# Up projections of a two-layer float32 transformer: each 512-column product issued as two halves of 256 columns

## The reference

```python
xn = layernorm(x)
x = x + L0_attn(xn) + L0_ffn(xn)   # causal attention, 32 heads of 16, 8 key/value heads, rotary
xn = layernorm(x)
x = x + L1_attn(xn) + L1_ffn(xn)   # causal sigmoid(4 * scores) without a softmax, 4 heads of 128

# L0_ffn, width 1792: each weight is multiplied elementwise by a product of rank 4
w_eff = w * (su @ sv)
out = down(silu(x @ gate_eff.T) * (x @ up_eff.T))
# L1_ffn, width 1376: the weight plus twice a product of rank 16
g = silu(lora(x, w1)) * lora(x, w3);  out = lora(g, w2)
```

## Time and profile before

| what | value |
|---|---|
| median of 3 timed executions | 708.31 us (707.09 to 709.48) |
| the profiled execution's own time | 710.41 us |
| its span, first to last instruction | 708.7 us |
| mean granted TensorE clock | 0.986 |
| matmuls recorded | 3606, as many weight loads |

### The profile page before, as it was taken

One profiled execution on the slowest core, in us unless ns is written; L12 is line 12 of the kernel. 1 busy time (PEld: TensorE's weight loads), 2 busy tenths in 40 slices (PEclk: granted clock), 3 DMA queues, 4 the chain that ended last, 5 costly groups with the idle time before them and its releaser, 6 DMA issues. The chain is left out here.

```text
span 708.7 us, 10147 instructions
## 1 busy us (share of the span) xinstructions
PE 684.1 (97%) x3606; PEld 518.3 (73%) x3606; DVE 417.5 (59%) x985; ACT 293.0 (41%) x552; POOL 236.5 (33%) x241
## 2 busy tenths in 40 slices
PE   8998999999999999999999999959999999999998
PEld 7787566666666666666687778847888788888886
DVE  6735865776767675566267662087666565565511
ACT  4212354555555544454434422245443344442321
POOL 4474022232222231222234625423233222322443
PEclk9998999999999999999999999978999999999999
DMA  9428714223313331321144520040010000102011
GB/s 290 116 89 226 153 32 123 69 73 92 74 44 74 74 74 44 74 79 57 43 141 156 181 86 0 1 122 31 31 59 31 31 30 31 60 30 60 16 59 60
DMA packets 23146, 55.19 MB, mean 78 GB/s; under 512 B 3732, under 2 KB 4088, under 8 KB 22040
## 3 DMA queue, kind: packets, MB, share of 16 engines
q1 hardware_dynamic: 22840, 54.41, 27.1%
q10 hardware_dynamic: 256, 0.13, 0.1%
HBM read 42.86 MB, written 11.54 MB: 77 GB/s over the span
## 5 line engine op out<-in xcount | busy, mean ns | idle before, releaser
L954 DVE CUSTOM_DVE_ANT_0 bank<-bank,mask 128x512 f32<-128x512 f32 (+3 forms) x256 | 118.4, 523 | 64.1 <-PE bank L1008 63.8
L214 POOL TENSOR_TENSOR up_w_lo<-up_w_eff,up_w_hi 128x512 fp32r<-128x512 f32 x50 | 65.8, 1323 | 123.0 <-ACT up_w_hi L210 122.9
L52 PE MATMUL bank<-x0T_hi,up_w_hi 128*128 128x512 f32 x224 | 96.9, 433 | 3.0 <-POOL up_w_lo L214 2.3
L383 POOL TENSOR_TENSOR down_h_lo<-hidden,down_h_hi 128x512 fp32r<-128x512 f32 x50 | 65.7, 1316 | 95.0 <-ACT down_h_hi L378 95.0
L908 ACT ACTIVATE probs<-bank 128x512 f32<-128x512 f32 x160 | 85.4, 597 | 28.5 <-PE bank L1030 25.8
L54 PE MATMUL bank<-x0T_lo,up_w_hi 128*128 128x512 f32 x224 | 89.5, 399 | 0.0
L53 PE MATMUL bank<-x0T_hi,up_w_lo 128*128 128x512 f32 x224 | 89.3, 399 | 0.0
L873 POOL TENSOR_SCALAR_AFFINE_SELECT probs<-probs 128x512 f32<-128x512 f32 x64 | 39.9, 635 | 124.3 <-ACT probs L908 124.1
L52 PE MATMUL bank<-down_w_hi,down_h_hi 128*128 128x512 f32 x200 | 78.3, 392 | 0.4 <-DVE bind_cols L1282 0.4
L53 PE MATMUL bank<-down_w_hi,down_h_lo 128*128 128x512 f32 x200 | 78.1, 390 | 0.0
L54 PE MATMUL bank<-down_w_lo,down_h_hi 128*128 128x512 f32 x200 | 78.0, 390 | 0.0
(11 more groups left out here) (144 smaller groups left out, 1277.4 us busy)
## 6 DMA issues: line engine op xcount, KB each, us to landing
w_raw<-in_w_gate_up SPq DMA_DIRECT2D x25, 512.0 KB, 4.2
w_raw<-in_w_down SPq DMA_DIRECT2D x25, 256.0 KB, 2.8
q_stack<-q_hi SPq DMA_DIRECT2D x32, 128.0 KB, 3.4
att<-att_T SPq DMA_DIRECT2D x16, 256.0 KB, 2.1
q_hi<-rope_hi SPq DMA_DIRECT2D x8, 256.0 KB
q_lo<-rope_lo SPq DMA_DIRECT2D x8, 256.0 KB
q_stack<-q_lo SPq DMA_DIRECT2D x16, 128.0 KB, 3.6
attention_or_xn<-att SPq DMA_DIRECT2D x16, 128.0 KB
```

What stands on the lines that cost most here:

```text
L52: pe.matmul(out, w_hi, m_hi, start=first, stop=False, skip_group_check=True)
L214: pool.tensor_tensor(self.half(self.w_lo[:, o % 2], k), self.half(self.w_eff, k), f32(self.half(self.w_hi[:, o % 2], k)), ALU.subtract).th ...
L383: pool.tensor_tensor(self.h_lo[:, k % 2, :], self.hid[:, o, b * S:(b + 1) * S], f32(self.h_hi[:, k % 2, :]), ALU.subtract).then_inc(self.h ...
L954: dve.tensor_tensor_reduce(out=own, in0=own, in1=e.mask[:, S - w:S], scale=1.0, scalar=NEG, op0=ALU.add, op1=ALU.max, accum_out=rmax[:, i, ...
```

## The change

A new helper `three_pass_halves` calls `three_pass` twice, first for the columns 0 to 255 of the bank and of the moving operand, then for 256 to 511, with the same stationary operands. Both versions of `pe_product` call it. Only the very first matmul of a bank keeps the flag `start`, and both halves carry `stop` at the end; the semaphore is raised by the last matmul of the second half.

```diff
+def three_pass_halves(pe, out, w_hi, w_lo, m_hi, m_lo, first, last):
+
+    for half in (slice(0, S // 2), slice(S // 2, S)):
+        done = three_pass(pe, out[:, half], w_hi, w_lo, m_hi[:, half], m_lo[:, half], first and half.start == 0, last)
+    return done
...
-        last = three_pass(pe, self.product_bank(o, b, k)[:, :], self.w_hi[:, o % 2, c, k, :], self.w_lo[:, o % 2, c, k, :],
-                          self.xT_hi[:, c, b * S:(b + 1) * S], self.xT_lo[:, c, b * S:(b + 1) * S],
-                          c == 0, c == NC - 1)
+        last = three_pass_halves(pe, self.product_bank(o, b, k)[:, :], self.w_hi[:, o % 2, c, k, :], self.w_lo[:, o % 2, c, k, :],
+                                 self.xT_hi[:, c, b * S:(b + 1) * S], self.xT_lo[:, c, b * S:(b + 1) * S],
+                                 c == 0, c == NC - 1)
```

## The result

The changed kernel takes 716.07 us (median of 4, 714.86 to 717.64) against 707.78 us for the kernel before in the same series. The ratio is 1.0115, with a 95% interval of 1.0083 to 1.0147. A second series of five executions beside thirteen of the kernel before gave 1.0121 (1.0102 to 1.0139). The forecast was 717.5 us and +9.2 us; measured are +8.3 and, from the second ratio, +8.6 us. The profiled execution took 714.96 us, its span is 713.2 us.

What follows compares the result with a forecast made beforehand. PE issuing matmuls back to back was taken to bound the kernel; +4.0 us (layer 0) + 5.7 (layer 1) - 0.5 (hidden) = +9.2 us on 708.31, so 717.5 us, 8-in-10 range 711.0 to 725 us.

Steps and rivals of the forecast that it cites:

- The bound: PE issues matmuls one behind the other, so a change in their distance reaches the end nearly in full; waits 16.6 us.
- The distance, 0.120 us: In long runs of up-projection halves, each 256-column matmul takes 0.120 us, so 0.240 us per former pass.
- the doubt about runs of three: Layer 1's three narrow passes show 0.117 us each, but a debt of 0.02 us may fall on the wide passes behind.
- the upper end, 0.123: A half in the up projections costs 0.123 us if the debt counts; the sum is then +16.7 us, 725 us.
- The small price: Rival: halves keep 0.117 us, layer 0 pays nothing, layer 1 +2.6 us, 710.6 us in all; chance 0.12.
- the faster way: Rival: halves in both layers go at the loads' 0.112 us, giving 699 us; chance 0.06.
- the slow pace in full: Rival: halves inherit layer 0's excess of 21 ns per matmul, 0.128 us each in both layers, 736 us; chance 0.06.
- the estimate from it: By the skill's issue-gap formula, halves cost 2.6 ns more per pass over 1179 passes, +3.1 us, 711.4 us.
- Layer 0, +4.0 us: 660 up-projection passes of layer 0 go from 0.234 to 0.240 us each, +4.0 us.
- Layer 1, +5.7 us: 519 up-projection passes of layer 1 go from 0.229 to 0.240 us each, +5.7 us.
- The hidden part, -0.5 us: PE's DMA waits absorb lost time: 0.3 us at five for `minus_max_rows`, 0.2 us at three for `weights_lo`.
- The lower clock: At 1.2 GHz halves cost nothing extra: 12 passes in layer 0 and 9 in layer 1 count 0.

Runs made afterwards that it cites:

- the down-projection run: Up projections whole again, the 600 passes of the two down projections in two pieces of 256 columns instead; 715.66 us, ratio 1.0104 to the kernel before.
- quarters: The changed kernel with each up product cut into four pieces of 128 columns instead of two of 256, 4800 matmuls; four executions took 1065.6 to 1095.3 us.
- thirds: The changed kernel with each up product cut into pieces of 172, 170 and 170 columns, 3600 matmuls; 851.75 us, ratio 1.2024 to the kernel before.

## Why the prediction was right

**The bound.** PE issues back to back and the end follows it: the price of halves in one layer, in the other and in the down projections each arrived at the end. The prediction's 16.6 us of waits are those of the six rows shown; all twelve in the list add up to 20.9 us, which changes nothing in the argument.

**The distance, 0.120 us.** Right, and the doubt about runs of three was justified: the earlier trace rows alone would have given 0.117, and long runs show 0.1194 to 0.120 in both layers and in the down projections. But 0.120 was taken midway between 0.117 and 0.123 and not worked out, so that it is right to 0.001 us is in part luck; the upper end, 0.123, is out as well. The small price (710.6 us) is out, and so are the faster way, which needed under 0.116, and the slow pace in full, 0.128: the slower pace of layer 0 at 512 columns is not passed on to halves. The Trainium skill ("TensorE: Matmul & The Clock Gate", Back-to-back issue gap) gives 109.2 ns for an isolated matmul of 256 columns by its formula, and the estimate from it was 711.4 us. This kernel, with a weight load for every matmul, shows 0.120 us and 716.07 us.

**Layer 0, +4.0 us.** Measured +3.9 by the layer alone (its interval is 2.6 to 5.2), +3.2 to +3.7 between marks against the second profile of the kernel before, and +3.4 by the estimate over eight traces. Right within what can be told.

**Layer 1, +5.7 us.** Between marks +4.5, and the forecast less its hidden part was +5.5: this term was a little too large. Halves at 0.1194 instead of 0.120 take 519 x 0.0012 = 0.6 us off. The waits for `weights_lo` fell from 2.3 to 1.8 us, 0.5 us where 0.2 had been expected. The timed runs of the layer alone say +5.2, with an interval of 3.7 to 6.7 that holds both figures.

**The hidden part, -0.5 us.** The step as put is not borne out in layer 0: the wait for `minus_max_rows` is 1.7 to 3.8 us with whole products and 1.6 to 2.7 with halves, so it varies from one execution to the next by more than the 0.3 us in question. The 3.8 us from which I argued belonged to a long execution. In layer 1 the mechanism shows, at 0.5 us: the wait for `weights_lo` is 2.3 us in all four traces with whole products there and 1.8 in all four with halves. In sum the term came out right by an exchange, which is luck.

**The lower clock.** Halves at 0.2133 us cost nothing, and in the two profiles of the changed kernel the stretches kept their lengths (7 us near 62 us, 14 near 468). They don't do so in every execution. With halves in layer 0 alone the clock was full behind the wait at 62 us, and low for 10 us later on, where PE waited 2.5 us for `up_gated`; with whole products in layer 0 (the down-projection run) the same was seen. From that first kernel:

```profile
62.00:69.00 7.00, 5.75 (x45) 5.50 (x45) 3.05 (x6) 1.54 (x2) 3.72 (x3) 1.00 0.96 272
69.00:82.00 13.00, 10.51 (x43) 8.91 (x43) 8.10 (x16) 6.63 (x9) 2.50 (x2) 0.61 0.94 215
```

The prediction had left such shifts in its range, at 1.5 us either way.

**What stays open.** Why a pass of 512 columns takes 0.234 us in layer 0 and 0.227 in the down projections, where halves take 0.120 everywhere, was not settled; nor why executions of one kernel differ by some 2.6 us in layer 0; nor whether the 13 ns above streaming come from the load or from the matmul, since no kernel here had one without the other.

## What to carry to other kernels

Read the cost of a matmul from the distance between starts in a long run of its own width, over whole rounds; a run of three beside wide ones flatters it. Here a matmul of N columns with its own weight load takes the larger of 0.112 us and its streaming time plus about 0.013 us at full clock (0.021 for whole passes in layer 0), so every cut of a 512-column product costs something, and pieces under about 240 columns ((0.112 - 0.013) x 2.4 GHz) cost a great deal more. Before a wait is counted as cover for new work, read it in a second profile of the unchanged kernel: here it was 3.8 us in one and 1.8 in the other. The same holds for a stage: the two profiles differ by 2.6 us in layer 0, most of the price that was looked for.

## What the runs showed of the hardware that was not expected

TensorE stayed at 1.2 GHz for about 99 us and again for over 200 us while it issued quarters and the attention work between them almost without a gap (PE is busy 97.6 of 99 us and 200.12 of 201), and for about 79 us with thirds in layer 0 (in layer 1 the thirds had the usual 14). The clock had fallen at the waits ahead of the first up products, 2.3 us long in layer 0. With whole products or halves in layer 0 it fell at the same wait, at one some 10 us later, or at both, and rose again each time after 3 to 10 us. A busy PE row alone did not bring the clock back here. Nor did quarters as such lower it: from 196 to 540 us it stayed full while they were issued. Which property of the work holds the clock down was not tested. The price of pieces that are too narrow is thus paid twice in these runs, once at the floor and once at the clock.
